# Decoder block over 128 sequences on one core: norms on ScalarE, a value product in fp32r parts, a re-ordered second half of the step

## What is computed

```python
# 1. self attention: one head of width 256, scores reshaped in bands
qkv  = LN(x) @ W_qkv + b_qkv
attn = softmax(sps_pro(q @ k.T / 4))          # sps_pro: times 0.1, 0.3, 1, 1.5 or 2 by the band of the score
x    = x + (attn @ v) @ W_proj + b_proj
# 2. gated cross attention on ctx, 8 heads of width 32
csum = cumsum(log_sigmoid(f_gate));  Dt = csum_i - csum_j + i_gate_j   (j <= i)
C    = (q_h @ k_h.T) * exp(Dt - max) / tau;   h = (C @ v_h) / max(|sum C|, exp(-max))
x    = x + groupnorm(h) * gn_w + gn_b
# 3. feed-forward 256 -> 1024 -> 256 with erf-gelu, plus a small product of token pairs in both layers
x    = x + ffn(LN(x))
```

## Time and profile before

| | |
|---|---|
| median of 3 runs | 1925.06 us (1924.22 to 1925.23) |
| the profiled execution's own time | 1924.64 us |
| its span in the trace | 1922.9 us |
| PE busy | 1809.3 us, 94% of the span |
| DVE busy | 1571.9 us, 82% |
| ACT busy | 1081.1 us, 56% |
| POOL busy | 335.0 us, 17% |
| mean granted TensorE clock | 0.987 |

### The profile page before, as it was taken

The page is one execution under the profiler, slowest core; times in us unless marked ns, Lnnn a source line. Parts: engine busy times, 40 slices in busy tenths (PEclk is TensorE's granted clock), DMA queues, the critical chain, the costliest instruction groups (busy, mean ns, idle before and its releaser), DMA issues.

```text
span 1922.9 us, 44190 instructions
## 1 busy us (share of the span) xinstructions
PE 1809.3 (94%) x14040; PEld 1362.2 (71%) x14040; DVE 1571.9 (82%) x4524; ACT 1081.1 (56%) x2440; POOL 335.0 (17%) x269
## 2 busy tenths in 40 slices
PE   5589999999999999999999999999999999999988
PEld 4457777777777777777777777777777777777766
DVE  6687888898888888888889888888888888888752
ACT  1355566555566655556655556665556665555552
POOL 2121121122022112112112102211211211210210
PEclk9789999999999999999999999999999999999999
DMA  4101111111111111111111111111111111111100
GB/s 119 31 28 26 35 45 47 39 42 25 44 36 47 47 36 46 25 35 45 47 38 44 24 42 39 47 47 36 46 25 35 45 47 37 45 24 39 32 15 25
DMA packets 205743, 75.57 MB, mean 39 GB/s; under 512 B 150273, under 2 KB 205186, under 8 KB 205714
## 3 DMA queue, kind: packets, MB, share of 16 engines
q1 hardware_dynamic: 205714, 75.21, 15.1%
HBM read 53.93 MB, written 16.78 MB: 37 GB/s over the span
## 4 chain that ended last, share of the span: by engine, by line
PE 77%; DVE 10%; issue 7%; ACT 5%; DMA 0%; SPq 0%; DVEq 0%; ACTq 0%
PE UA L1376 17%; PE UB L1376 5%; PE TB L1453 3%; PE GT L1386 3%; DVE bands L965 3%; PE TA L1343 3%; PE TA L1453 3%; PE UB L1318 3%; PE TA L1283 3%; PE TA L1184 3%; PE TB L1184 3%; PE UA L1318 3%; ACT QKs L694 3%; PE PV L1318 2%; PE UB L1420 2%
## 5 line engine op out<-in xcount | busy, mean ns | idle before, releaser
L1376 PE MATMUL UA<-W2f,hs_all 128*128 128x256 f32 x1536 | 350.8, 381 | 3.8 <-DVE ot L1022 3.1
L1376 PEld LDWEIGHTS UA<-W2f,hs_all 128*128 128x128 f32 x1536 | 286.5, 190 | 67.0 <-ACT hs_all L704 14.1
L1039 DVE TENSOR_TENSOR C<-qT,QKs 128x512 f32<-128x512 f32 x256 | 166.2, 690 | 113.7 <-ACT qT L713 104.4
L598 POOL TENSOR_TENSOR Ng<-HT,gnw_b 128x256 f32<-128x256 f32 x128 | 105.4, 824 | 823.2 <-ACT HT L726 823.2
L579 POOL TENSOR_TENSOR xg<-x,gnb_b 128x1024 f32<-128x1024 f32 x32 | 83.9, 2621 | 682.6 <-ACT ot L668 645.6
L1376 PE MATMUL UB<-W2f,hs_all 128*128 128x256 f32 x512 | 115.8, 379 | 0.0
L612 ACT ACTIVATE lv<-ve 128x4 f32<-128x4 f32 x95 | 19.1, 202 | 164.2 <-DVE ve L831 164.2
L694 ACT ACTIVATE QKs<-TA 128x512 f32<-128x512 f32 x64 | 38.4, 600 | 125.3 <-PE DD L1343 125.3
L1376 PEld LDWEIGHTS UB<-W2f,hs_all 128*128 128x128 f32 x512 | 95.0, 190 | 11.7
L1343 PEld LDWEIGHTS TA<-xn2T,ctxT 32*128 32x128 f32 x512 | 63.3, 190 | 43.6 <-issue 41.1
L1343 PE MATMUL TA<-xn2T,ctxT 32*128 32x128 f32 x512 | 74.9, 286 | 19.3 <-DVE acs L969 17.1
(11 more groups left out here) (328 smaller groups left out, 5146.2 us busy)
## 6 DMA issues: line engine op xcount, KB each, us to landing
xin<-x SPq DMA_DIRECT2D x32, 512.0 KB, 3.4
ctxn<-ctx SPq DMA_DIRECT2D x32, 512.0 KB, 3.5
bands<-ctx SPq DMA_DIRECT2D x256, 64.0 KB, 1.9
out<-ot SPq DMA_DIRECT2D x32, 512.0 KB, 3.0
Ev<-xn SPq DMA_DIRECT2D x512, 1.0 KB
hs_all<-L_ffn_W SPq DMA_DIRECT2D x4, 512.0 KB, 8.4
E<-xn SPq DMA_DIRECT2D x128, 16.0 KB
T<-tok SPq DMA_DIRECT2D x128, 8.0 KB, 1.7
```

The lines of the kernel that those rows point to most:

```text
L598: pool.tensor_tensor(Ng[:, b, :].rearrange("p (k n) -> p k n", k=2), HT[:, b % 2, :, 0:P], gnw_b[:, :].rearrange("p (k n) -> p k n", k=2), ...
L1039: dve.tensor_tensor(C[:, b % 2, :, half], dx[hf].rearrange("p (h i) -> p h i", h=HEADS), QKs[:, b, :, half], ALU.mult)\
L1376: ins = pe.matmul(OB[b][:, 0:D], hs_all[:, k, b * S:(b + 1) * S], W2f[:, k, :], start=(i == 0), stop=(i == KH - 1))
```

## The change

1. Value product: `values(b)` issues six fp32r matmuls of 256 columns in place of two fp32 ones. The weight Wvp becomes Wvh (rounded to fp32r) and Wvl (the rest), made in the set-up; the copy on ACT now writes pxh in fp32r, and a new DVE operation `px_rest(m)` (PSUM minus pxh, twice per step) writes pxl. pxh and pxl use the memory of xn3h and xn3l. `values` waits for both rests.
2. Norms: `ln_apply` goes to ACT (Identity with scale `rs` and bias `shift` per partition). DVE makes `shift` in `ln_scale`, one more small operation per norm. On ACT it stands behind `hs(3)` for norm 0, and behind `ln_root` for norms 2 and 1.
3. PE order: the first half of `down(1)` stands ahead of `values(0)`; the first half of `down(2)` ahead of `turn_xn1`.
4. Gates: gabs and lsig lie in PSUM (bank GT, columns 128 to 383). acs has three rows of 128; the running maximum is now taken by a scan that reads acs and DD, and `acs_ok` follows it; the copy of the old row into `am` is gone. The band comparison stands behind `rows`.
5. QKs: `keep_qk` copies the banks in the order DD, QQ, TA, GT, and `decay(0, 0)` and `decay(0, 1)` wait for one of these copies each, where `decay(0, 0)` waited for all eight.
6. DVE order: the 32x32 transpose of the context blocks stands right behind `ln_stats(0)`, and its input has a buffer of its own; `weigh_qk(1, .)` stands ahead of `ln_scale(0)`.
7. DMA and POOL: SP issues the eight block loads behind the T rows at the start of the step; the context is loaded into vc itself, behind the E rows. POOL subtracts in place and then writes the ones with a second small operation.

```diff
@@ sync
                 if FFN.on(it):
                     t_rows(it)
+                if SELF.on(it):
+                    sp.wait_ge(ctxT_ok.h, ctxT_ok.at(it, 0))
+                    for h in range(HEADS):
+                        sp.dma_start(ctx_blocks[...], c_blocks[it][...]).then_inc(blocks_loaded.h, 16)
...
-                if SELF.on(it):
-                    sp.wait_ge(vc_ok.h, vc_ok.at(it, 1))
-                    sp.dma_start(ctxn[:, :, :], c_g[it]).then_inc(ctx_loaded.h, 16)
...
                 if CROSS.on(it):
                     e_rows(it)
+                if SELF.on(it):
+                    sp.wait_ge(pv_mm.h, pv_mm.at(it, G))
+                    sp.dma_start(vc[:, :, :], c_g[it]).then_inc(ctx_loaded.h, 16)
@@ scalar
+            def ln_apply(i, it, X, Xn, free):
+                act.wait_ge(rs_ok[i].h, rs_ok[i].at(it, 1))
+                for f, k in free:
+                    act.wait_ge(f.h, f.at(it, k))
+                for b in range(G):
...
+                    ins = act.activation(dst, src, ACT.Identity, bias=shift[i][:, b:b + 1], scale=rs[i][:, b:b + 1])
+                ins.then_inc(xn_ok[i].h, 1)
...
-                    for r in range(4):
+                    for r in (3, 1, 0, 2):
...
-                    act.activation(pxT[:, m, :], TAB[m][:, :], ACT.Copy).then_inc(px_ok.h, 1)
+                    act.activation(pxh[:, m, :], TAB[m][:, :], ACT.Copy).then_inc(px_ok.h, 1)
...
                     hs(3)
+                if coming:
+                    ln_apply(0, it, xin, xn1, [(score_mm, 1), (px_mm, 2)])
+                if cross:
                     ht(3)
...
                     ln_root(2, it)
+                    ln_apply(2, it, x3, xn3, [(xn3T_mm, 2), (e_loaded, 0), (ev_loaded, R * G * 16)])
...
                     ln_root(1, it)
+                    ln_apply(1, it, x2, xn2, [(xn2T_mm, 2), (x2_ok, G)])
@@ vector
+                dve.scalar_tensor_tensor(shift[i][:, :], mean[i][:, :], -1.0, rs[i][:, :], ALU.mult, ALU.mult)\
+                   .then_inc(rs_ok[i].h, 1)
...
-                if own:
-                    dve.wait_ge(sc_ok.h, sc_ok.at(it, 1))
-                    band_lo = v.mark(dve.tensor_scalar(band_a[:, :], sc[:, :], BANDS[0], 0.3, ALU.is_ge, ALU.mult))
-                    band_hi = v.mark(dve.tensor_scalar(band_b[:, :], sc[:, :], BANDS[3], None, ALU.is_gt))
...
-                    dve.tensor_copy(acs[:, :], DD[0:32, 0:2 * P]).then_inc(acs_ok.h, 1)
+                    link(dve.tensor_copy(acs[:, 0:2, :].rearrange("p a n -> p (a n)"), DD[0:32, 0:2 * P]))
+                    dve.tensor_tensor_scan(acs[:, 2, :], acs[:, 1, :], DD[0:32, P:2 * P], -3e38,
+                                           ALU.max, ALU.max).then_inc(acs_ok.h, 1)
...
+                def px_rest(m):
+                    dve.wait_ge(px_ok.h, px_ok.at(it, m + 1))
+                    dve.tensor_tensor(pxl[:, m, :], TAB[m][:, :], pxh[:, m, :].bitcast(F32), ALU.subtract)\
+                       .then_inc(pxl_ok.h, 1)
@@ tensor
                     pe.wait_ge(dexp_ok.h, dexp_ok.at(it, max(k - 1, 0)))
+                    if k < 2:
+                        pe.wait_ge(QKs_ok.h, QKs_ok.at(it, 5 + k))
                     if k == 0:
-                        pe.wait_ge(QKs_ok.h, QKs_ok.at(it, 8))
...
-                    pe.wait_ge(px_ok.h, px_ok.at(it, 2))
-                    for k in range(KD):
-                        ins = pe.matmul(TAB[b // 2][...], pxT[:, k, b * S:(b + 1) * S],
-                                        Wvp[:, k, :], start=(k == 0), stop=(k == 1))
+                    pe.wait_ge(pxl_ok.h, pxl_ok.at(it, 2))
+                    for px, w in ((pxh, Wvh), (pxh, Wvl), (pxl, Wvh)):
+                        for k in range(KD):
+                            ins = pe.matmul(TAB[b // 2][...], px[:, k, b * S:(b + 1) * S],
+                                            w[:, k, :], start=(px is pxh and w is Wvh and k == 0),
+                                            stop=(px is pxl and k == 1))
...
+                if ffn:
+                    down(1, range(0, KH // 2))
                 if own:
                     values(0)
...
-                    down(1)
+                    down(1, range(KH // 2, KH))
                     adapt(1)
+                if ffn:
+                    down(2, range(0, KH // 2))
                 if coming:
                     turn_xn1(it)
                 if ffn:
-                    down(2)
+                    down(2, range(KH // 2, KH))
                     adapt(2)
```

More of the change, by code:

```diff
@@ L187, in build @@
         cut = sb("cut", [P, 1])
+        one = sb("one", [P, 1])
         lntau = sb("lntau", [P, 1])
@@ L268, in build @@
         rs = [sb(f"rs{i}", [P, G]) for i in range(3)]
+        shift = [sb(f"shift{i}", [P, G]) for i in range(3)]
         def bank(name):
@@ L853, in _ @@
             ln_scale(0, done)
-            ln_apply(0, xin, xn1)
+            for b in range(G):
+                ins = dve.tensor_scalar(xn1[:, b, :], xin[:, b, :], mean[0][:, b:b + 1], rs[0][:, b:b + 1],
+                                        ALU.subtract, ALU.mult)
+            ins.then_inc(xn_ok[0].h, 1)
             dve.wait_ge(s_load_a, 16 * LOADS_A)
@@ L1089, in step @@
                     o_out(0)
+                if own:
+                    px_rest(0)
                 if cross:
@@ L1092, in step @@
                 if own:
[L1093 to L1096 removed]
+                    px_rest(1)
+                if own:
                     dve.wait_ge(probs_ok.h, probs_ok.at(it, 1))
@@ L1364, in step, with down @@
                     up_adapter(1)
-                def down(b):
-                    if b == 1 or b == 3:
+                def down(b, chunks=range(KH)):
+                    if 0 not in chunks:
+                        pass
+                    elif b == 1 or b == 3:
                         pe.wait_ge(ot_ok.h, ot_ok.at(it, (b + 1) // 2))
```

119 lines of the change are left out of this document (54 added, 65 removed).

## The result

The changed kernel takes 2005.73 us (median of 4 runs, 2003.27 to 2006.29), the kernel before beside it 1924.64 (1922.93 to 1925.23): a ratio of 1.042, 95% interval 1.0402 to 1.0438. It is slower by 81 us. The forecast was 1869, the range 1842 to 1902.

What follows compares the result with a forecast made beforehand. PE was taken to bound the kernel, by matmul time and its waits. Gates 34.7, C 9.3 and value product 24.6 us gained, norms 13.0 lost, net 55.6: 1924.6 - 55.6 = 1869 us, range 1842 to 1902.

Steps and rivals of the forecast that it cites:

- The gates' chain: DVE's scan runs free beside POOL; PE's waits at sums (0.48 us) and qk(0) (0.64) go: 1.12 us per step.
- The QKs order: Copies ahead of decay: no gain, since down(0) behind it starts 0.05 us behind the gelu of up(4).
- C for pv(1): DVE weighs C(1) before it scales norm 0, so PE's wait at pv(1) goes: 0.30 us per step.
- The value product: 24 fp32r records at 0.12 us replace 3.44 us of fp32, and the wait of pv(3) goes: 0.77 us per step.
- The norms on ACT: ACT's applications, 1.55 us per norm, make xn3T's copy 0.9 us late; PE loses 0.45 us per step, bounds 0 and 0.9.
- Halving down changes the place of matmuls and not their number … All zero.: Splitting down on PE, with the DMA, POOL and set-up changes, was put at zero gain or loss.
- ACT and the scan take more: Rival: scan stays stalled (15 us) or ACT's norms delay PE by 0.9 us (13 us); near 1885, both near 1897; chance 0.2.
- the chance of 0.05 for slower: Rival at the value product: short fp32r matmuls cost what long ones do, 14 us slower, 1939 us; chance 0.05.
- my last sign: Sign of being wrong: ACT runs without idle time in the last 8 us of the step.

Runs made afterwards that it cites:

- Experiment 11: Core with gabs and lsig in SBUF again and two band operations ahead of the copy of the sums: 1954.69 us, ratio 1.0156.
- experiment 1: The changed kernel with all three norm applications back on DVE at their old places: 1913.66 us, ratio 0.9939 to the kernel before.
- experiment 6: The changed kernel with one wait added on POOL, so that xg starts only when DVE's Ef is done: 1969.84 us, ratio 1.0236.
- core: The changed kernel with all three norm applications back on DVE, everything else of the change kept: 1913.66 us.
- experiment 9: Core with down(1) and down(2) whole at their old places: 1913.02 us, ratio 0.9939.
- experiment 12: Core with the last turn_h on PE between values(2) and values(3): 1890.67 us, ratio 0.9823.
- 15: Core with turn_h(3) earlier, o_out(2) moved, unused shifts dropped, two of norm 2's four applications on ACT, xg waiting for Ef: 1876.79 us.

## Why the prediction was wrong

The measured step is 59.3 us, the predicted one 55.1. The steps of the prediction that failed are the price of the norms on ACT and the zero for the halved `down`. In the order of the prediction:

- *The gates' chain*, 1.12 us per step. Mechanism right in each row: the scan takes 0.42 us under POOL, PE waits at neither `sums` nor `qk(0)`. From the start of `up_adapter(0)` to that of `qk(0)` the step got 0.72 us shorter (3.58 to 2.86 us), not 1.12: PE reached `up(4)` before the gelu of `up(0)` was through and waits 0.21 us there, and `sums` starts 0.44 us behind the side-by-side matmuls where I had 0.32. Experiment 11 shows that the two places of the gates' chain matter, but its 1.3 us holds a scan that the kernel before has elsewhere. The rule of the Trainium skill that I had weighed (GPSIMD Engine Reference, section 1, Specifications: contention "with two SBUF inputs") is borne out by the scan, and in a way that I did not use by Ef, whose Er and E are both in SBUF.
- *The QKs order*, nothing. Right by the rows, though it was not taken out by itself. `down(0)` starts 0.05 us behind its gelu (44.63 + 0.69):

```profile
1044.63 0.69 ACT L724 ACTIVATE hs_all<-UA,b1c 128x512 f32<-128x512 f32 x1
...
1045.37 0.92 PE L1395 MATMUL UA<-W2f,hs_all 128*128 128x256 f32 x3 [0.24 <-ACT hs_all L724]
```

- *C for pv(1)*, 0.30 us. Right: the wait is gone; from `pv(0)` to `pv(1)` it is 0.37 us less (2.95 to 2.58).
- *The value product*, 0.77 us. Sized too high, 0.5 to 0.56. The spacing of 0.12 is right within a piece, but each of its three pieces starts with 0.1 to 0.2 us more. The rule of the Trainium skill (TensorE: Matmul & The Clock Gate, where it stands in the section The mechanism) that a weight load overlaps "only when row_grp differs" would have given 0.213 us per record; the rows show 0.118 and speak against it.
- *The norms on ACT*, a loss of 0.45 us, bounds 0 and 0.9. **This step failed**, and in three ways. First the size: 0.47 us came from an Identity on 128 columns that reads PSUM and has one operand per partition, with 128 columns more. One of 256 columns from SBUF with two such operands takes 0.59, and with a stride of 4 it takes 0.84; the two norms hold ACT for 5.1 us and not 3.1. Second the bound of 0.9, which was my own estimate of the lateness and no bound. Both together cost 0.8 us at the turning of xn3 and 0.9 at Z per step over experiment 1. Third, what a late step does to others: with Z late, xg starts ahead of Ef, Ef takes 2.06 us in the mean, `up(4)` waits, and in a third of the steps the clock falls. By experiment 6 this is 36 us of the 92.
- *"Halving down changes the place of matmuls and not their number … All zero."* This is the second step that failed. The place mattered: it moves the last `turn_h` later by 0.9 us (5.10 us behind the start of the last `decay` before, 6.01 in core), which I had noted under the norms and followed along ACT only. What counts is the work that PE has left from there to `gram`: 19.17 us before, 17.51 in core, 1.66 less. DVE's chain from `turn_h` to Z is as long as it was (18.0 and 18.1 us without the gap ahead of Z), and its slack in the kernel before was 0.7 us: 0.24 that DVE idled ahead of Z, and 0.44 by which Z was ready early. The rest is the wait for Z of 1.04 us that stays even with the norms on DVE. Of the 1.6 us per step that the other parts did save, it takes back 1.0; experiment 9 moves the wait elsewhere by putting `down` back, and experiment 12 shortens it by moving `turn_h` alone, for 23 us.

The sum of the steps: predicted without the norms 54.7; less gain at the gates 0.4; at the values about 0.2; the wait for Z 1.0: 56.3, and core has 56.4. The norms on ACT: turning of xn3 0.8, Z 0.9, Ef with `up(4)` 0.9, the clock 0.2 in the mean: 2.8 more, and the changed kernel has 59.3. The rival "ACT and the scan take more" had the mechanism at 0.2 and ended at 1897, since it let each loss take its own bound and no more. No rival was slower through ACT, and the price of ACT's share was not bounded above by any row: that is what the chance of 0.05 for slower got wrong. Nor did my last sign fire, ACT without idle time in the last 8 us of the step: it idles 1.10 us ahead of norm 1's application, for DVE's `shift`, since the work goes back and forth between the two engines.

## What to carry to other kernels

- When work moves between engines, draw the whole chain from the last product to the first that waits for its result, and count the gaps of every engine in it. The smallest gap, with what the last result is early, is the most that anything ahead may be late for nothing: here 0.24 and 0.44 us. A saving on TensorE behind the head of such a chain is only waited for; moving the head itself earlier (`turn_h` by one value product) gave 23 us for no work.
- DVE's Ef takes 0.49 us if it starts ahead of POOL's xg and 2.4 us if it starts up to 0.3 us behind it. Such an order can flip by 0.1 us. If one side is in the critical chain, write the order down with a wait, as experiments 6 and 15 do, before judging any other edit by its time.
- A single step of a loop is a sample. The low clock stood in one step of three, and the wait of 1.15 us at `up(4)` in the others.
